# Transformer layer with 64 experts: the last attention taken by query tile, and nine experts' weight loads moved

## The chip, the cores and the metric

One core of a Trainium2 chip runs the whole program. The metric is the device time of one execution in microseconds, as a median over runs. The engines are TensorE (PE), VectorE (DVE), ScalarE (ACT), GpSimd (POOL) and SyncE (SP); SyncE issues the plain transfers, GpSimd the indirect ones.

## The reference

x is 4 x 256 x 256. A modulation from a small matrix gives shift, scale and gate for two sub-layers. Float32 throughout.

```python
h = layernorm(x) * (1 + ca) + sa
x = x + ga * attention(h)            # 16 heads of 16, rotary, causal, 256 x 256 weights
h = layernorm(x) * (1 + cb) + sb
x = x + gb * experts(h)
...
# experts: x has 1024 tokens
probs = softmax(h @ router_weight.T)             # 64 experts
topw, topi = top_k(probs, 8); topw = topw / sum(topw)
pos = rank of each (token, expert) among the expert's tokens, in token order
xe[e, pos] = h (pos < 128 only)                  # capacity 128
y = sum over k of topw * down_e(silu(g) * u),  g, u = split(xe @ gate_up_e)   # 256 -> 2 x 96 -> 256
```

The rank in token order makes the slot number of a token depend on all tokens before it, so the tiles of 128 tokens have their slots made in order.

## The kernel before

A batch is 256 tokens, two tiles of 128 (TPB = 2); there are B = 4 batches, eight tiles. The attention stage is a software pipeline written out by hand for each engine: a round `it` does the second half of batch it - 1 (softmax, values, output projection, second norm, router, top 8, slots) beside the first half of batch `it` (projections, rotary, transposes, and the scores whose maxima the softmax subtracts). Engines meet at semaphores only. Each one's instructions run in the order of the text, so a wait holds all that is written behind it on that engine.

**The last attention** (batch 3) has no batch beside it. On TensorE `attend` (line 943) makes, for each of four groups of four heads, the transposed scores of both query tiles in three chunks (two pairs of heads with 256 queries against key tile 0, and four heads with 128 queries against key tile 1), and one group later the products with the values (L959); ScalarE's `softmax` makes the exponentials (L664) and copies two groups at a time to the SBUF (L671). `att_transposes` (L988) turns the result to tokens by rows, VectorE's `attention_out` divides, `out_transposes` (L996) and `o_proj` (L1005) project, `residual` adds and takes statistics, `rstd` and `finish_rstd` make 1/sqrt, `h2_normalise`, `h2_transposes` (L1013) and `h2_copy` make the modulated norm, `router` (L1029) the logits, `rows_transposes` (L1020) the rows to be scattered, `picks` and `slots` (L1354 to L1388) the top 8 and the slot numbers, with `ranks` (L1038) between them. In this tail the two tiles are handled apart but side by side: on VectorE in the order residual 0, finish 0, residual 1, finish 1, picks 0, slots 0, picks 1, slots 1. `keep_warm` issues products whose result nobody reads (L852): four and two within the tail, 30 after the last slot numbers, and three after the wait for seven tiles' scatters.

**The scatters.** GpSimd writes each tile's rows to the slots of their experts in DRAM with eight indirect transfers (L596), one for each of the eight choices; those of batch 2 run beside the last attention, each behind a wait (`beside_last_attention`) that spaces them out. Transfers of the last tile count on a semaphore of their own (`g_last`), all others on `g_scat`.

**The experts.** For each of 64 experts SyncE loads 128 slot rows (`load_slots`, L448, eight buffers), TensorE transposes them (L1146; for the first five experts, whose slots can hold rows of the last tile, it adds those from the SBUF by a product with a 0/1 matrix, L1143 to L1148), multiplies (L1157), transposes (L1165) and multiplies again (L1171). GpSimd adds the result to one of three sums in DRAM (L616, L619), each add after the one before on the same sum; results wait in a ring of 16. The nine last experts are added by products on TensorE (L1199). At the end the sums are loaded and folded by VectorE.

**The weights.** All experts' weights live in one SBUF tensor, `arena`, whose second half (experts 32 to 63) is scratch of the attention stage until its parts come free. Of experts 32 to 63, seven were loaded at the start of what the last values products free (AFTER_PV = 7: 32 to 38), nine (39 to 47, up to AFTER_QK = 16) after the last slot numbers, and the others before. SyncE's order around this is:

```python
sp.wait_ge(p_pv, 4 * B)
sp.dma_start(code_table, ...)
load_experts(EARLY, AFTER_PV, s_lw[1])
sp.wait_ge(v_slot, B * TPB)
load_experts(EARLY + AFTER_PV, AFTER_QK - AFTER_PV, s_lw[2])
sp.wait_ge(g_scat, 16 * K * (B * TPB - 1))
```

Then come the first five slot loads, the wait for `g_last`, three more, and the rest, each behind the step that frees its buffer.

## Time and profile before

| | us |
|---|---|
| median of 3 runs | 336.37 (331.1 to 338.41) |
| the profiled execution | 329.7 |
| its span, first to last instruction | 327.9 |
| TensorE busy | 288.1 (88%) |
| VectorE busy | 206.2 (63%) |
| ScalarE busy | 158.8 (48%) |
| GpSimd busy | 158.9 (48%) |

The mean granted clock of TensorE is 0.952 of full speed. The span has two stages: the attention, to about 174, and the experts, from 189.73 to the end; between them all computing engines but GpSimd are idle or run products that nobody reads. Busy shares are means over both, so a part of the kernel is judged by the order of time in it. Every time below is in us from the start of the span. An engine's idle time stands in brackets with what ended it; "issue" is time in which it waited for nothing that the profile shows.

### The profile page before, as it was taken

The numbers are of one execution on the slowest core, as the hardware profiler recorded it, in microseconds if no ns is written. First come the engines' busy times: TensorE is split into PE (matmuls) and PEld (weight loads), VectorE is DVE, ScalarE is ACT, GpSimd is POOL, SyncE is SP. The second block draws the span as 40 slices with busy tenths as digits, with TensorE's granted clock in tenths as the row PEclk, the third lists the DMA queues.
The fourth block names the chain that finished last, engine by engine and source line by source line (L and its number), as shares of the span: only waits on it lengthen the run. The fifth ranks groups of instructions, "written<-read, shape, count | busy, mean of one in ns | idle before, by whom it ended". The sixth has DMA issues, their size and how long they took to land.

```text
span 327.9 us, 7233 instructions
## 1 busy us (share of the span) xinstructions
PE 288.1 (88%) x2084; PEld 213.0 (65%) x2084; DVE 206.2 (63%) x640; ACT 158.8 (48%) x461; POOL 158.9 (48%) x156
## 2 busy tenths in 40 slices
PE   7999999899889898969658389999999999999990
PEld 3468477466646674646333089788888887778880
DVE  3296677778677967740552027677767679993186
ACT  3437288428743584436241015566666666592000
POOL 2800000003455455655737732687887788887300
PEclk9998999999999999599967969999999999999997
DMA  7880399999999998812977953699999988866972
GB/s 219 266 274 3 48 335 336 351 381 239 286 308 270 289 241 262 223 69 80 227 212 223 289 155 108 139 152 160 158 156 165 188 148 151 107 72 71 222 239 96
DMA packets 63594, 64.89 MB, mean 198 GB/s; under 512 B 4880, under 2 KB 60375, under 8 KB 63569
## 3 DMA queue, kind: packets, MB, share of 16 engines
q1 hardware_dynamic: 52864, 49.39, 54.3%
q0 software_dynamic: 10704, 15.20, 25.7%
q8 instruction: 12, 0.20, 0.3%
q14 instruction: 14, 0.11, 0.1%
HBM read 36.26 MB, written 28.84 MB: 199 GB/s over the span
## 4 chain that ended last, share of the span: by engine, by line
PE 60%; issue 14%; DVE 9%; DMA 7%; ACT 6%; SPq 2%; POOL 0%; another core or an unknown queue 0%; ACTq 0%; DVEq 0%; POOLq 0%
PE bank L1157 12%; PE bank L1171 7%; PE bank L899 6%; PE bank L1146 3%; PE bank L975 3%; PE bank L911 3%; PE bank L973 3%; PE bank L959 3%; PE bank L930 2%; DMA sum<-kz,stage 2%; PE bank L970 2%; PE bank L927 2%; PE bank L1165 2%; PE bank L1005 2%; DVE arena L1552 2%
## 5 line engine op out<-in xcount | busy, mean ns | idle before, releaser
L596 POOL DMA_INDIRECT slot_rows<-stage x48 | 47.9, 998 | 38.3 <-issue 10.9
L1157 PE MATMUL bank<-arena,stage 128*128 (+1 forms) x256 | 53.5, 331 | 0.6 <-ACT stage L800 0.6
L616 POOL DMA_INDIRECT sum<-kz,stage x26 | 40.1, 1543 | 9.5 <-issue 6.6
L800 ACT ACTIVATE stage<-bank 128x256 f32<-128x256 f32 x64 | 24.6, 384 | 38.1 <-PE bank L1148 22.6
L1157 PEld LDWEIGHTS bank<-arena,stage 128*128 128x128 f32 x256 | 40.3, 191 | 1.7 <-issue 0.8
L1171 PE MATMUL bank<-arena,stage 96*128 (+1 forms) x128 | 40.4, 397 | 0.1
L1299 DVE TENSOR_REDUCE rmax<-bank 128x2 f32<-128x512 f32 (+1 forms) x48 | 30.6, 685 | 5.9 <-PE bank L930 4.6
L616 POOL DMA_INDIRECT sum<-stage x17 | 26.4, 1554 | 6.8 <-issue 5.0
L664 ACT ACTIVATE arena<-bank 128x512 f32<-128x512 f32 x48 | 26.7, 599 | 6.0 <-PE bank L975 5.3
L583 POOL COPY stage<-slot_idx 128x16 uint32<-128x16 uint32 x2 | 0.4, 197 | 59.9 <-DVE slot_idx L1388 59.9
L899 PE MATMUL bank<-arena 128*128 128x512 f32 (+1 forms) x64 | 25.8, 528 | 2.9 <-ACT arena L647 2.9
L852 PE MATMUL bank<-onesb 128*128 128x512 bf16 x67 | 21.3, 474 | 7.7 <-DMA slot_rows<-rows,slot_idx 4.9
L1510 DVE SCALAR_TENSOR_TENSOR stage<-stage,bank 128x96 f32<-128x96 f32 x64 | 16.2, 253 | 16.8 <-ACT stage L810 11.2
L975 PE MATMUL bank<-stage 128*128 128x256 bf16 (+1 forms) x128 | 24.6, 246 | 0.0
L973 PE MATMUL bank<-arena,kz 128*128 128x256 f16 (+1 forms) x128 | 24.6, 246 | 0.0
L807 ACT ACTIVATE stage<-bank 128x96 f32<-128x96 f32 x64 | 16.1, 251 | 17.2 <-PE bank L1157 9.9
L1199 PE MATMUL bank<-arena 128*128 128x256 bf16 x216 | 23.7, 271 | 0.0
L1146 PE MATMUL bank<-cst,stage 128*128 128x128 f32 x118 | 22.9, 275 | 0.1
L1199 PEld LDWEIGHTS bank<-arena 128*128 128x128 bf16 x216 | 20.9, 97 | 2.8
L1171 PEld LDWEIGHTS bank<-arena,stage 96*128 96x128 f32 x128 | 19.1, 189 | 3.9 <-ACT stage L817 0.3
L1146 PEld LDWEIGHTS bank<-cst,stage 128*128 128x128 f32 x118 | 16.2, 141 | 7.5 <-issue 2.1
L596 POOL DMA_INDIRECT slot_rows<-rows,slot_idx x16 | 16.2, 1013 | 9.2 <-DVE slot_idx L1388 4.6
(199 smaller groups left out, 603.2 us busy)
## 6 DMA issues: line engine op xcount, KB each, us to landing
slot_rows<-zero_row SPq DMA_DIRECT2D x8, 1040.0 KB, 12.6
stage<-slot_rows SPq DMA_DIRECT2D x64, 130.0 KB
arena<-in_gate_up SPq DMA_DIRECT2D x8, 768.0 KB
sum<-zero_row SPq DMA_DIRECT2D x3, 1152.0 KB, 12.6
arena<-in_gate_up SPq DMA_DIRECT2D x4, 864.0 KB
arena<-in_down SPq DMA_DIRECT2D x4, 768.0 KB
arena<-sum SPq DMA_DIRECT2D x12, 256.0 KB, 5.3
arena<-in_gate_up SPq DMA_DIRECT2D x4, 672.0 KB
```

Source lines behind the costliest of these rows:

```text
L596: pool.indirect_dma_start(slot_rows, bass.IndirectOffsetOnAxis(ap=idx[:, t, k:k + 1], axis=0), src[:, t, :], None, bounds_check=SLOTS - 1, ...
L616: pool.indirect_dma_start(sums[a], where, ye_ring[e % RING], None, bounds_check=ACCROWS - 1, oob_is_err=True, compute_op=ALU.add).then_inc ...
L664: nc.scalar.activation(dst, bank[4 + n % 3][:, :], ACT.Exp, scale=SCALE).then_inc(a_exp, 1)
L800: nc.scalar.activation(xeT[:, j % 2, :], bank[j % 2][:, 0:HC * CAP], ACT.Copy).then_inc(a_xeT, 1)
L899: mm(dst, h1T[:, k, t * P:(t + 1) * P], wqkv_sb[:, k, c0:c1], start=k == 0, stop=False)
L973: mm(view[:, i, :], kz[:, h, kt * P:(kt + 1) * P], qT[:, h // 2, kt * P:S], start=False, stop=False, skip_group_check=True)
L975: last = mm(view[:, i, :], pickb[:, h, :], negT[:, kt * P:S], start=False, stop=i == len(heads) - 1, skip_group_check=True)
L1146: last = nc.tensor.transpose(dst, xe[:, j, k * P:(k + 1) * P], ident)
L1157: last = mm(bank[2 + q % 2][:, 0:GU + 1], xeT[:, q % 2, k * CAP:(k + 1) * CAP], expert_w[:, s - 1, k * (GU + 1):(k + 1) * (GU + 1)], start ...
L1171: mm(bank[6 + q % 2][:, 0:H], hidT[:, q % 2, :], expert_w[0:I, s - 3, HC * (GU + 1):EW], start=True, stop=True).then_inc(p_ye, 1)
L1199: last = mm(dst, picked[:, n, of:of + P], y[:, n, :], start=n == 0 and y is own_high, stop=n == NPICK - 1 and y is own_low)
L1299: V.tensor_reduce(rmax[:, qt, h0:h0 + 2 * nh - 1:2], src, AX.X, ALU.max).then_inc(v_max, 1)
```

## The change

The last attention goes by query tile. The scores are made in twelve chunks of four heads by 128 queries: four for tile 0 (key tile 0 only), then eight for tile 1. The values, the copy, the transposes, the projection and the residual of tile 0 are issued between tile 1's chunks. Exponentials go to six buffers in place of probT's two groups (`probs_last`). On VectorE tile 0's picks and slots stand ahead of tile 1's residual, on ScalarE its rows and sums ahead of tile 1's estimate. Six warm-up products within the tail are gone; the 30 and the three stay. GpSimd's waits for batch 2's eighth to twelfth scatter name later events. Of the nine experts' weights, four are loaded after tile 1's projection, and five, one by one, behind the first five slot loads of the third round (`load_eight(2, ...)`), which with round 1 is written out of the loop; TensorE waits for these five before step 40, so that round 4 is written out too. `wo_sb` changes places with `rope2` in the scratch, so that what the first 11 late experts overwrite (AFTER_O = 11) is no longer used once the last projection is done.

```diff
...
+        def probs_last(n):
+
+            return probT[:, :, :].rearrange("p a c -> p (a c)")[:, (n % 6) * 512:(n % 6 + 1) * 512]
+
         def tiles(ts):
...
             load_experts(EARLY + AFTER_QK, ANYTIME - AFTER_QK, s_lw[0])
-            sp.wait_ge(p_pv, 4 * B)
+            sp.wait_ge(p_pv, 4 * B + 4)
             sp.dma_start(code_table, code_row.rearrange("o (e c) -> o e c", c=CAP).broadcast_to([P, FIRST, CAP])).then_inc(s_cr, 16)
             load_experts(EARLY, AFTER_PV, s_lw[1])
+            sp.wait_ge(p_o, B + 1)
+            load_experts(EARLY + AFTER_PV, AFTER_O - AFTER_PV, s_lw[2])
             sp.wait_ge(v_slot, B * TPB)
-            load_experts(EARLY + AFTER_PV, AFTER_QK - AFTER_PV, s_lw[2])
...
-            def load_eight(i):
+            def load_eight(i, weights=0):
                 for j in range(GRP):
                     load_slots(i, j, False)
-
-            with sp.Fori(1, 6) as i:
+                    if j < weights:
+                        load_experts(EARLY + AFTER_O + j, 1, s_lw[3])
+
+            load_eight(1)
+            load_eight(2, AFTER_QK - AFTER_O)
+            with sp.Fori(3, 6) as i:
                 load_eight(i)
...
                     pool.wait_ge(p_s2, 12 * c + 2 * n - 3)
-                elif n in (8, 9):
-                    pool.wait_ge(p_pv, 4 * c + n - 5)
+                elif n == 8:
+                    pool.wait_ge(p_o, B)
+                elif n == 9:
+                    pool.wait_ge(p_pv, 4 * c + 7)
                 elif n == 10:
...
                 elif n == 11:
-                    pool.wait_ge(p_attT, B)
+                    pool.wait_ge(p_attT, B + 1)
                 elif n == 12:
-                    pool.wait_ge(p_o, B)
+                    pool.wait_ge(p_o, B + 1)
                 elif n == 13:
...
             one_round(B - 1, False)
-            softmax(B - 1, None)
-            for t in ALL:
-                att_copy((t,), B + t, t)
+
+            def last_exp(n):
+                if n >= 6:
+                    act.wait_ge(p_pv, 4 * (B - 1) + (n - 5 if n < 10 else 5))
+                act.wait_ge(p_s2, 12 * (B - 1) + n + 1)
+                nc.scalar.activation(probs_last(n), bank[4 + n % 3][:, :], ACT.Exp, scale=SCALE).then_inc(a_exp, 1)
+
+            def last_att_copy(t):
+                act.wait_ge(p_pv, 4 * (B - 1) + 4 * (t + 1))
+                nc.scalar.activation(att_sb[:, t, :], bank[(7, 2)[t]][:, :], ACT.Copy).then_inc(a_att, 1)
+
+            for n in range(6):
+                last_exp(n)
+            last_att_copy(0)
+            for n in range(6, 10):
+                last_exp(n)
+            att_copy((0,), B, 1)
+            last_exp(10)
+            last_exp(11)
+            last_att_copy(1)
             rstd((0,), B)
+            att_copy((1,), B + 1, 0)
             h2_normalise(B - 1, (0,), B)
             h2_copy(B - 1, (0,), B, 0)
+            rows_copy(B - 1, (0,), B, 0)
+            exp_sums(B - 1, (0,), B)
             rstd((1,), B + 1)
             h2_normalise(B - 1, (1,), B + 1)
-            rows_copy(B - 1, (0,), B, 0)
-            exp_sums(B - 1, (0,), B)
             h2_copy(B - 1, (1,), B + 1, 1)
...
             one_round(B - 1, False)
-            attend(B - 1)
-            att_transposes(B - 1)
-            for t in ALL:
-                out_transposes(B - 1, (t,), t)
-                o_proj((t,), B + t, t)
-            keep_warm(4, bank[4])
+            def last_scores(n):
+                g, t, kt = (n, 0, 0) if n < 4 else ((n - 4) // 2, 1, n % 2)
+                if n >= 3:
+                    pe.wait_ge(a_exp, 12 * (B - 1) + n - 2)
+                view = bank[4 + n % 3][:, :].rearrange("p (h q) -> p h q", q=P)
+                if t == kt:
+                    mm(view, identb, maskTb[:, None, :].broadcast_to([P, 4, P]),
+                       start=True, stop=False, skip_group_check=True)
+                for i, h in enumerate(groups[g]):
+                    mm(view[:, i, :], kz[:, h, kt * P:(kt + 1) * P], qT[:, h // 2, t * P:(t + 1) * P],
+                       start=t != kt and i == 0, stop=False, skip_group_check=True)
+                    last = mm(view[:, i, :], pickb[:, h, :], negT[:, t * P:(t + 1) * P],
+                              start=False, stop=i == 3, skip_group_check=True)
+                last.then_inc(p_s2, 1)
+
+            def last_values(t, g):
+                pe.wait_ge(a_exp, 12 * (B - 1) + (g + 1 if t == 0 else 2 * g + 6))
+                for kt in range(t + 1):
+                    slot = probs_last(g if t == 0 else 4 + 2 * g + kt)
+                    for i, h in enumerate(groups[g]):
+                        last = mm(bank[(7, 2)[t]][32 * i:32 * i + 32, g * P:(g + 1) * P], v_aug[:, kt, h, :],
+                                  slot[:, i * P:(i + 1) * P], start=kt == 0, stop=kt == t, skip_group_check=True)
+                last.then_inc(p_pv, 1)
+
+            def last_att_transposes(t):
+                pe.wait_ge(a_att, 2 * (B - 1) + t + 1)
+                for g in range(4):
+                    last = nc.tensor.transpose(bank[(0, 5)[t]][:, g * P:(g + 1) * P],
+                                               att_sb[:, t, g * P:(g + 1) * P], ident)
+                last.then_inc(p_attq, 1)
+
+            pe.wait_ge(a_negT, B)
+            for n in range(3):
+                last_scores(n)
+            pe.wait_ge(v_rank, B)
+            last_values(0, 0)
+            last_scores(3)
+            last_values(0, 1)
+            last_scores(4)
+            last_values(0, 2)
+            last_scores(5)
+            last_values(0, 3)
+            last_scores(6)
+            last_scores(7)
+            last_att_transposes(0)
+            last_values(1, 0)
+            last_scores(8)
+            last_scores(9)
+            last_values(1, 1)
+            out_transposes(B - 1, (0,), 1)
+            last_scores(10)
+            last_scores(11)
+            o_proj((0,), B, 0)
+            last_values(1, 2)
+            last_values(1, 3)
+            last_att_transposes(1)
+            out_transposes(B - 1, (1,), 0)
+            o_proj((1,), B + 1, 1)
             h2_transposes(B - 1, (0,), B, 0)
...
             rows_transposes((0,), 0)
-            keep_warm(2, bank[3])
+            ranks((0,), B, 0)
             h2_transposes(B - 1, (1,), B + 1, 1)
-            ranks((0,), B, 0)
             router((1,), B + 1, 1)
...
                 pe.wait_ge(s_lw[n], 16 * 3)
-            with pe.Fori(EARLY // GRP, E // GRP) as i:
+            for j in range(GRP):
+                expert_steps(EARLY // GRP, j, False, False)
+            pe.wait_ge(s_lw[3], 16 * 3 * (AFTER_QK - AFTER_O))
+            with pe.Fori(EARLY // GRP + 1, E // GRP) as i:
                 for j in range(GRP):
...
             one_round(B - 1, False)
             clear()
-            attention_out(B - 1)
-
+            attention_out(B - 1, (0,), (0, 5))
             residual(B - 1, (0,), B, 0)
             finish_rstd((0,), B)
+            attention_out(B - 1, (1,), (0, 5))
+            picks(B - 1, (0,), B, 0)
+            slots(B - 1, (0,), B, 0)
             residual(B - 1, (1,), B + 1, 1)
             finish_rstd((1,), B + 1)
-            picks(B - 1, (0,), B, 0)
-            slots(B - 1, (0,), B, 0)
             picks(B - 1, (1,), B + 1, 1)
...
```

## Rows read from the trace of the kernel before

**Rows 1.** The chain of waits from 140 to 200: start us, us, what.

```profile
158.29 15.24 issue
...
177.48 9.35 issue
186.82 1.88 DMA stage<-slot_rows
```

**Rows 2.** GpSimd's instructions in order of time: start us, us, engine, line.

```profile
165.36 0.97 POOL L596 DMA_INDIRECT slot_rows<-stage  x1 [0.31 <-issue]
170.92 0.97 POOL L596 DMA_INDIRECT slot_rows<-rows,slot_idx  x1 [4.58 <-DVE slot_idx L1388]
...
180.50 0.97 POOL L596 DMA_INDIRECT slot_rows<-rows,slot_idx  x1 [0.30 <-issue]
...
190.72 0.97 POOL L596 DMA_INDIRECT slot_rows<-rows,slot_idx  x1 [0.31 <-issue]
```

**Rows 3.** SyncE's slot loads issued from 192 to 193: duration ns min/median/max.

```profile
L448 SPq DMA_DIRECT2D stage<-slot_rows x1: 328/328/328, 192.8 to 192.8; - x1
```

**Rows 4.** Stretch, us, busy us of PE, PEld, DVE, ACT, POOL, clock, DMA share, GB/s.

```profile
161.00:163.00 2.00, 1.94 (x9) 1.08 (x9) 1.32 (x7) 0.41 (x3) 1.16 (x2) 1.00 1.09 385
...
176.00:177.00 1.00, 1.00 (x4) 0.35 (x3) 0.00 (x0) 0.00 (x0) 0.69 (x2) 0.50 0.80 264
177.00:178.00 1.00, 1.00 (x6) 0.49 (x5) 0.00 (x0) 0.00 (x0) 0.70 (x2) 0.98 1.02 347
...
193.00:194.00 1.00, 1.00 (x8) 1.00 (x6) 0.46 (x3) 0.00 (x0) 0.00 (x0) 0.50 0.15 22
194.00:195.00 1.00, 1.00 (x7) 1.00 (x8) 0.31 (x3) 0.40 (x2) 0.00 (x0) 0.94 0.94 253
...
209.00:212.00 3.00, 2.94 (x18) 2.54 (x18) 2.07 (x9) 1.94 (x8) 2.64 (x2) 1.00 0.73 132
...
221.00:230.00 9.00, 9.00 (x58) 7.99 (x57) 7.20 (x26) 5.83 (x25) 7.18 (x6) 1.00 0.92 156
```

**Rows 5.** GpSimd's first, fifth and last adds, TensorE's late products, columns as rows 2.

```profile
200.88 1.00 POOL L619 DMA_INDIRECT sum<-stage  x1 [8.79 <-DVE stage L1520]
...
209.05 1.57 POOL L616 DMA_INDIRECT sum<-stage  x1 [1.47 <-issue]
...
304.89 1.54 POOL L616 DMA_INDIRECT sum<-kz,stage  x1 [0.30 <-issue]
...
296.03 23.75 PE L1199 MATMUL bank<-arena 128*128 128x256 bf16 x216
```

**Rows 6.** TensorE's instructions in order of time, columns as in rows 2.

```profile
154.92 0.86 PE L959 MATMUL bank<-arena 128*32 128x256 f32 x16 [0.72 <-ACT arena L664]
156.50 1.09 PE L988 MATMUL bank<-cst,arena 128*128 128x128 f32 x8 [0.72 <-ACT arena L671]
...
158.88 1.13 PE L1005 MATMUL bank<-arena 128*128 128x256 f32 x4 [0.47 <-ACT arena L688]
...
163.94 0.44 PE L1013 MATMUL bank<-cst,arena 128*128 128x128 f32 x2 [0.56 <-issue]
...
173.56 8.35 PE L852 MATMUL bank<-onesb 128*128 128x512 bf16 x30 [1.65 <-issue]
...
189.73 0.77 PE L1143 MATMUL bank<-cst,stage 128*128 128x128 f32 x2 [1.80 <-issue]
```

**Rows 7.** Weight loads of line 959, from 143 to 170: count, busy us, mean ns.

```profile
L959 PEld LDWEIGHTS bank<-arena 128*32 128x32 f32 x64 | 1.7, 109 | 2.0 <-ACT arena L664 1.0
```

**Rows 8.** VectorE's instructions in order of time, columns as in rows 2.

```profile
160.26 0.42 DVE L1328 TENSOR_TENSOR arena<-bank,arena 128x256 f32<-128x256 f32 x1 [1.73 <-PE bank L1006]
...
167.48 0.23 DVE L1354 MAX8 top<-bank 128x8 f32<-128x64 f32 x1 [1.16 <-PE bank L1029]
...
169.86 0.17 DVE L1388 TENSOR_SCALAR slot_idx<-code 128x8 uint32<-128x8 f32 x1
...
173.33 0.17 DVE L1388 TENSOR_SCALAR slot_idx<-code 128x8 uint32<-128x8 f32 x1
```

13 lines of the change are left out of this document (7 added, 6 removed).

## The prediction

> **What bounds the kernel now.** I first read the chain of waits around the last attention [rows 1]. From 158.29 it holds no computing engine: SyncE's queue sits still for 15.24 us until the last tile's slot numbers exist, issues the nine late experts' loads, sits still again for 9.35 us until seven of the eight tiles' rows have been scattered, and only then loads the first slots. GpSimd in order of time gives the cause [rows 2]: sixteen scatters of batch 2 run to 166.33, the queue is empty for 4.58 us, and the sixteen of batch 3 start at 170.92, one each 1.28 us, the eighth ending at 181.47 and the last at 191.69. So three things are in series: the tail of the attention, the scatters, and a landing. The landing is read from two places: the eighth scatter ended at 181.47 and SyncE went on at 186.82, 5.35 us later; the last ended at 191.69 and SyncE went on at 192.8, 1.1 us later [rows 1 to 3]. Between the two the traffic differs: the DMA engines were full from 177 on (1.02), and nearly empty at 193 (0.15) [rows 4].
>
> After that the end is set by GpSimd's adds, 55 in all, 1.54 us each with 0.30 between: from 209.05 to 304.89 there are 50 steps of 1.845 us, which is 92.2 of 95.8 us [rows 5]. TensorE ends its late products at 319.78 [rows 5]. Both ends move with the start of the experts.
>
> **Part 1, the attention by query tile.** Scores and values are as much work as before: 12 blocks of 128 columns for each group of four heads, 12 exponentials and two copies of 512 columns on ScalarE. New is the order. Tile 0's transposes, out transposes and projection now stand before tile 1's last values: four and two transposes of 0.11 us (eight take 0.88 and a tail) and 1.17 for the projection with its bias, 1.8 us of TensorE [rows 6]. The last values ended at 155.78; in the new order 157.6. The leg from there until VectorE reads a projection took 155.78 to 160.26, 4.48 us [rows 6, 8]; for tile 1 it has four transposes fewer (0.44) and waits once more: VectorE has finish_rstd of tile 0 ahead of it, whose estimate stands on ScalarE behind the second copy of the attention, which I put at 0.65 us. So tile 1's projection is done at 157.6 + 4.48 - 0.44 + 0.65 = 162.3.
>
> The smaller values products need 96 weight loads in place of 64. The row says 109 ns each [rows 7], and 16 of them lie within the 0.86 us of a group [rows 6], where one after the other they would take 1.74; so they overlap, and I take 0, with 32 x 0.109 = 3.5 us as the other bound. A rule speaks against the change here: the Trainium skill (TensorE: Matmul & The Clock Gate, The mechanism, in the part on packing) has weight loads overlap running products only when the row group differs, and here it is the same; by the rule up to 3.5 us would be paid, and the sum below would be -1.0. The trace does not agree.
>
> **Part 2, tile 0's back half.** Its h2_transposes follow the second projection at once, where they now start at 163.94 behind four warm-up products. From them to the slot numbers it takes until 170.03, 6.1 us, of which 1.16 is a wait before 167.48 that nothing in the trace explains [rows 6, 8]. New: 162.35 + 4.9 to 6.1, so 167.2 to 168.4. GpSimd gets free later: its waits for batch 2 are re-spread, and the twelfth needs tile 1's projection. Add 0.9 (what the first scatter took to start behind slot numbers ready at 170.03) and four scatters, 5.1 us: free at 168.3. So the first scatter of batch 3 starts at 168.3 to 169.3; I take 168.7, 2.2 us earlier. The eighth ends at 168.7 + 7 x 1.277 + 0.97 = 178.6, the last at 188.8.
>
> **Part 3, tile 1's back half** now stands whole behind tile 0's slots on VectorE. From residual to slots it takes 160.26 to 170.03, 9.8 us, for tile 0 now. Without the 1.16 wait and with 0.4 for products at the low clock: 9.0, bounds 8.6 and 10.2 (the wait stays). Last slots: 167.8 + 9.0 = 176.8 (175.8 to 178.6), against 173.50 now [rows 8]. **They become later by 3.3 us**, and what is queued behind them matters: the 30 warm-up products on TensorE, 8.35 us [rows 6], the first of them at the low level of the clock (0.50, 1.2 GHz, until 177; 2.4 GHz after [rows 4]); TensorE will have been as idle before them. GpSimd needs these slots at 168.7 + 10.2 = 178.9 and is not held by them.
>
> **Part 4, the weights.** Four experts (1.2 MB) go out at 162.3 behind the seven that already fill the DMA engines then (1.09 at 161 to 163 [rows 4]); only scatters that nobody waits for share that time. At the eighth scatter's end the engines are quiet, and I take the landing of the quiet case, 1.1 us (bounds 1.1 and 5.35): rows of seven tiles are in at 179.7. TensorE is at its warm-up products until 176.8 + 0.06 + 8.35 = 185.2, and after three more (0.64) starts at 185.9. So the landing leaves the path, but **the warm-up products are late next**. The gain at TensorE's start is 189.73 - 185.9 = 3.8 us (2.1 to 4.8). In exchange no idle lies between them and the experts: at present TensorE runs from 189.73 to 194 at 0.50 [rows 4, 6], 4.3 us that are 2.1 at 1.00. Gain 2.0 (0 to 2.1). Slots 5 and up wait for the last scatter, 188.8 + 1.1, and a load of 1.9 [rows 1]: 191.8, wanted after five steps of 1.5 us or more, 193.4 at the earliest: hidden.
>
> Five experts (1.5 MB) go into the second round of slot loads. Fifteen more issues on SyncE at 0.33 us [rows 3] are 5 us, and the slot loads are eight steps (12 us) ahead, so they hide. The traffic is 1.5 MB at the 347 GB/s of a full stretch [rows 4], 4.2 us of all engines, where they are 0.73 busy and GpSimd waits 1.47 us once already; later they are at 0.92 [rows 4, 5]. An add waits for the one three before it, so a later landing is paid. Bounds 0 and 4.2; I take 1.3, what is left when the idle quarter of 12 us takes its share.
>
> The extra unrolled eight on TensorE and the wait for the fourth weights semaphore cost nothing: the weights are there some 25 steps before. wo_sb changes its place only.
>
> **Sum**, against the profiled execution's own 329.7 us (span 327.9 and 1.8 around it): -3.8 - 2.0 + 1.3 = -4.5, so 325.2. The median of the runs shown is 336.37 (331.1 to 338.41), 6.7 above that execution; the same shift puts the median at 331.8, I say 331.5.
>
> **Rivals.**
> One, all bounds are kind: slots at 175.8 and TensorE at 184.9 (4.8), clock 2.1, no contention, and half a us of the wait before 209.05 goes: 7.4 gained, 329. For it: the 1.16 wait looks like an accident. Against: traffic is not free. Chance 0.22.
> Two, the change moves the first scatter but not the experts: tile 1's tail is long, slots at 178.6 or later, TensorE at 187.6, gain 2.1 + 2.0 - 1.3 = 2.8, 333.6. For it: the clock is low for all of its products. Chance 0.15.
> Three, the weight loads of the values products are not hidden: 3.5 later, gain 1.0, 335.4. Against it stands the row above. Chance 0.05.
> Four, slower: the five loads among the adds. If they make a landing 4.25 us later, as the nine did to the eighth scatter (5.35 against 1.1), a chain of three adds pays it once a round, and the loads span two to three rounds: 8.5 to 12.8 us, less the 5.8 gained before, is 2.7 to 7 slower, 339 to 343. It decides from 1.4 rounds on. Against it: each load is 0.29 MB, not 2.65 at once, with 1.5 us between. Chance 0.08. The Trainium skill (DMA: Bandwidth & Descriptors, Issuing engines are not separate DMA queues) has the transfers of all engines interleave on the same 16, which is what this rival needs.
> The forecast itself: 0.50.
>
> **Numbers.** Runs of this kernel differ by 2% among themselves, and 2% (6.7 us) is about what tells a change from none. Rival one is over it, with some of the forecast's edge: faster 0.27. Rival four is beyond it on the other side: 0.08. The rest, 0.65, is within. Range: the forecast with its bounds is 328.5 to 334; out to rivals one and two and the spread of the runs it is 326 to 337.
>
> **What would show it.** In the changed profile: tile 1's projection at 162 to 163; the first scatter from rows at 168.3 to 169.3, with no gap of 4.6 before it; last slot numbers at 176 to 178; SyncE's first slot load 1.1 us behind the eighth scatter, near 180; TensorE's 30 warm-up products ending after that, and the experts starting at 185 to 187 at a clock of 1.00; 55 adds at 1.85 with no longer waits near the tenth. I am wrong if the warm-up products are not what the experts wait for, if the clock is 0.50 at the experts' start, or if the adds stretch.

## The result, and the profile after

In 20 runs of each, the changed kernel took 336.19 us in the median (331.51 to 338.72) and the kernel before 334.55 (328.66 to 338.41). Some executions of every kernel lie more than 1.5% above its fastest; the ratios here and below leave them out, the medians do not. The ratio is 1.0118, 95% interval 1.0071 to 1.0164: slower by about 4 us (the medians differ by 1.6), where I had forecast 4.5 to 5 us faster. Repeated in three more comparisons the ratio was 1.0175 [1.0111, 1.0239], 1.0144 [1.0063, 1.0224] and 1.0216 [1.0139, 1.0294]. The profiled execution took 337.46 us with a span of 335.6 and a mean granted clock of 0.927 (before 329.7, 327.9, 0.952).

The chain of waits of the changed kernel (start us, us, what) already says where to look:

```profile
156.78 3.95 another core or an unknown queue
...
164.49 2.07 PE bank L1035 x4
...
170.79 5.01 issue
...
181.43 10.21 PE bank L882 x33
192.64 0.27 PE bank L1225
192.91 1.83 issue
194.90 1.24 issue
196.31 0.33 PE bank L1224 x2
```

SyncE is gone from it, as intended [rows 1]. In its place stand the warm-up products (L882), which I had forecast, and four pieces in which an engine waits, the first and the last two of which I had not. GpSimd in order of time (start us, us, engine, line), the last scatter of batch 2, the first, eighth and last of batch 3, then the first and last add:

```profile
171.53 0.98 POOL L608 DMA_INDIRECT slot_rows<-stage  x1 [0.30 <-issue]
173.07 0.97 POOL L608 DMA_INDIRECT slot_rows<-rows,slot_idx  x1 [0.56 <-issue]
...
182.03 0.97 POOL L608 DMA_INDIRECT slot_rows<-rows,slot_idx  x1 [0.30 <-issue]
...
192.27 0.97 POOL L608 DMA_INDIRECT slot_rows<-rows,slot_idx  x1 [0.30 <-issue]
...
205.77 1.00 POOL L631 DMA_INDIRECT sum<-stage  x1 [12.13 <-DVE stage L1604]
...
311.09 1.54 POOL L628 DMA_INDIRECT sum<-kz,stage  x1 [0.30 <-issue]
```

The 4.58 us gap ahead of batch 3 is gone [rows 2], yet its first scatter came at 173.07, not 168.7. And from the last scatter's end to the first add it took 12.5 us (205.77 less 193.24), where it had taken 9.2 [rows 2, 5]. SyncE goes on 1.3 us after the eighth scatter's end, as forecast:

```profile
184.31 20.08 SPq L454 DMA_DIRECT2D stage<-slot_rows  x12
```

TensorE in order of time, from the last values to the first experts (L1224 to L1238):

```profile
156.83 1.08 PE L1157 MATMUL bank<-arena 128*32 128x128 f32 x32
...
161.40 1.12 PE L1164 MATMUL bank<-cst,arena 128*128 128x128 f32 x4 [3.49 <-ACT arena L799]
...
181.43 10.21 PE L882 MATMUL bank<-onesb 128*128 128x512 bf16 x33 [1.65 <-DVE slot_idx L1472]
191.48 0.38 PE L1224 MATMUL bank<-cst,stage 128*128 128x128 f32 x2
...
192.15 0.28 PE L1225 MATMUL bank<-kz,rows 128*128 128x128 f32 x1
192.64 0.27 PE L1225 MATMUL bank<-kz,rows 128*128 128x128 f32 x1 [0.22 <-issue]
194.74 0.17 PE L1229 MATMUL bank<-kz 128*128 128x3 f32 x1 [1.83 <-issue]
196.14 0.17 PE L1229 MATMUL bank<-kz 128*128 128x3 f32 x1 [1.24 <-issue]
196.17 0.47 PE L1224 MATMUL bank<-cst,stage 128*128 128x128 f32 x2
```

There are two holes. **Hole B**: inside the first expert TensorE stands still for 0.22, 1.83 and 1.24 us between products that wait for no data and no buffer (the slots are long there); it runs on from 196.14, 2.9 us after the last scatter's end. **Hole A**: the 32 last values products end at 157.9 by their modelled end, but the two engines that wait for their count both go on at 160.75 (ScalarE's copy, and SyncE's load of the code table):

```profile
160.75 0.35 SPq L441 DMA_DIRECT2D kz<-in_code_row  x1
160.75 0.60 ACT L799 ACTIVATE arena<-bank 128x512 f32<-128x512 f32 x1 [3.97 <-remote]
```

So it looks as if TensorE itself was late with the last of them, whose ends the profile only models. The stretches (us, busy of PE, PEld, DVE, ACT, POOL, clock, DMA share, GB/s) show what the clock did then, and the adds:

```profile
161.00:163.00 2.00, 1.12 (x4) 0.72 (x4) 1.05 (x6) 0.64 (x3) 0.00 (x0) 0.50 0.40 106
163.00:176.00 13.00, 5.73 (x18) 3.32 (x19) 4.68 (x22) 3.46 (x10) 8.18 (x9) 0.50 1.04 291
...
182.00:192.00 10.00, 10.00 (x38) 4.27 (x36) 0.28 (x3) 0.00 (x0) 7.81 (x8) 0.73 0.48 145
...
221.00:230.00 9.00, 9.00 (x56) 7.67 (x55) 6.63 (x25) 5.94 (x25) 6.16 (x4) 1.00 1.04 247
```

After hole A the clock is at 0.50 (1.2 GHz) from 161 on, where before it was 1.00 at 161 to 163 [rows 4]; tile 1's projection takes 2.07 us where 1.13 was its price [rows 6]. At 221 to 230 the engines carry 247 GB/s, 156 before [rows 4], which fits the five moved loads.

### The profile page after: what moved, and what is told of

The parts are those of the page before. It is cut to its first block, busy times and chain, and to the rows that moved or that the text cites. A ratio compares the mean times of both kernels' runs of the same rounds, so it can differ in the third digit from the quotient of the medians.

```text
span 335.6 us, 7275 instructions
## 1 busy us (share of the span) xinstructions
PE 288.7 (86%) x2138; PEld 214.8 (64%) x2138; DVE 205.5 (61%) x640; ACT 158.6 (47%) x461; POOL 158.4 (47%) x156
## 4 chain that ended last, share of the span: by engine, by line
PE 60%; DVE 12%; issue 12%; ACT 8%; DMA 5%; another core or an unknown queue 1%; SPq 1%; POOL 0%; ACTq 0%; DVEq 0%; POOLq 0%
PE bank L1238 11%; PE bank L1252 7%; PE bank L929 6%; PE bank L1227 3%; PE bank L882 3%; PE bank L941 3%; ACT arena L676 2%; DMA arena<-sum 2%; PE bank L960 2%; PE bank L1246 2%; PE bank L1059 2%; PE bank L1035 2%; PE bank L957 2%; DVE arena L1636 2%; DVE rmax L1383 2%
## 5 line engine op out<-in xcount | busy, mean ns | idle before, releaser
L1238 PE MATMUL bank<-arena,stage 128*128 (+1 forms) x256 | 54.0, 333 | 0.7 <-ACT stage L830 0.7
L1238 PEld LDWEIGHTS bank<-arena,stage 128*128 128x128 f32 x256 | 40.8, 193 | 1.6 <-issue 1.1
L1252 PE MATMUL bank<-arena,stage 96*128 (+1 forms) x128 | 40.1, 395 | 0.0
L1227 PE MATMUL bank<-cst,stage 128*128 128x128 f32 x118 | 22.8, 274 | 0.0
L882 PE MATMUL bank<-onesb 128*128 128x512 bf16 x61 | 20.4, 500 | 2.7 <-DVE slot_idx L1472 1.7
L676 ACT ACTIVATE arena<-bank 128x512 f32<-128x512 f32 x36 | 20.0, 599 | 3.2 <-PE bank L1005 2.7
L960 PE MATMUL bank<-kz,arena 128*128 128x128 f16 (+1 forms) x128 | 18.9, 255 | 0.0
L1005 PE MATMUL bank<-stage 128*128 128x256 bf16 (+1 forms) x96 | 18.4, 246 | 0.0
L1003 PE MATMUL bank<-arena,kz 128*128 128x256 f16 (+1 forms) x96 | 18.4, 246 | 0.0
```

The lines of the kernel that those rows point to most:

```text
L676: nc.scalar.activation(dst, bank[4 + n % 3][:, :], ACT.Exp, scale=SCALE).then_inc(a_exp, 1)
L882: mm(idle[:, :], onesb, onesb[:, None, :].broadcast_to([P, 4, P]), start=True, stop=True)
L960: last = mm(view[:, i, :], qT[:, h // 2, qt * P:(qt + 1) * P], kz[:, h, 0:w], start=False, stop=i == len(heads) - 1, skip_group_check=True)
L1227: last = nc.tensor.transpose(dst, xe[:, j, k * P:(k + 1) * P], ident)
L1238: last = mm(bank[2 + q % 2][:, 0:GU + 1], xeT[:, q % 2, k * CAP:(k + 1) * CAP], expert_w[:, s - 1, k * (GU + 1):(k + 1) * (GU + 1)], start ...
L1252: mm(bank[6 + q % 2][:, 0:H], hidT[:, q % 2, :], expert_w[0:I, s - 3, HC * (GU + 1):EW], start=True, stop=True).then_inc(p_ye, 1)
```

## The experiments

Single executions start the last attention at different times (138.4 to 146.2 us over all profiles, in no order), so all profiles are compared from t0, ScalarE's copy that opens the last attention (143.99 before, 144.15 after). "Comparison" is one set of kernels timed together with the kernel before; the holes turned out to depend on it.

| kernel | comparison, median of before | median | ratio [95%] |
|---|---|---|---|
| c0, changed again | I, 328.65 | 333.86 | 1.0175 [1.0111, 1.0239] |
| e1, before + weights only | I | 333.26 | 0.9996 [0.9934, 1.0059] |
| e2, attention only | I | 335.80 | 1.0209 [1.0152, 1.0266] |
| e3, 12 late warm-ups | I | 335.33 | 1.0157 [1.0081, 1.0233] |
| e4, slot loads all last | II, 327.81 | 337.62 | 1.0311 [1.0234, 1.0387] |
| e5, 96 instructions more, earlier | II | 332.74 | 1.0195 [1.0107, 1.0283] |
| e6, 180 more, in late warm-ups | II | 337.92 | 1.0299 [1.0198, 1.0400] |
| e7, residual 1 first | II | 333.38 | 1.0168 [1.0076, 1.0260] |
| f1, before + e6's padding | III, 322.89 | 323.28 | 1.0015 [0.9976, 1.0055] |
| f2, 128 more on ScalarE | III | 325.58 | 1.0087 [1.0039, 1.0136] |
| f3, 128 more on TensorE | III | 322.68 | 0.9952 [0.9902, 1.0002] |
| f4, no late warm-ups | III | 318.61 | 0.9847 [0.9787, 0.9908] |
| g0, changed again | IV, 332.58 | 335.97 | 1.0144 [1.0063, 1.0224] |
| g1, f4 again | IV | 330.90 | 1.0083 [1.0012, 1.0153] |
| g2, before, no late warm-ups | IV | 327.29 | 0.9891 [0.9800, 0.9982] |
| g3, e1, no late warm-ups | IV | 334.40 | too spread for a ratio |
| h1, one last scatter of eight | V, 329.41 | 329.48 | 1.0039 [0.9994, 1.0084] |
| h2, changed again | V | 334.92 | 1.0216 [1.0139, 1.0294] |

The steps, in us from t0, each from one profile; "forecast" is the prediction less 143.99, its last two entries following from its sum:

| | before | forecast | after | h2 | h1 | f2 | f3 | f4 | g1 |
|---|---|---|---|---|---|---|---|---|---|
| tile 1's projection done | 18.4 | 18.3 | 22.7 | 22.8 | 22.7 | 18.7 | 18.7 | 18.7 | 22.7 |
| first scatter of batch 3 | 26.9 | 24.7 | 28.9 | 29.0 | 28.9 | 24.6 | 24.6 | 24.6 | 28.9 |
| last slot numbers | 29.5 | 32.8 | 37.2 | 37.3 | 37.2 | 32.9 | 32.5 | 32.5 | 37.2 |
| last scatter's end | 47.7 | 44.8 | 49.1 | 49.1 | 40.1 | 44.8 | 44.8 | 44.8 | 49.1 |
| TensorE's first expert | 45.7 | 41.9 | 47.3 | 47.2 | 45.9 | 41.6 | 41.6 | 38.1 | 42.6 |
| first add | 56.9 | 51.1 | 61.6 | 61.7 | 54.9 | 50.6 | 50.6 | 49.6 | 58.7 |
| last add, less first | 104.0 | 105.3 | 105.3 | 104.1 | 104.3 | 104.3 | 102.9 | 102.9 | 104.4 |

**Which part costs it (c0, e1, e2).** e1 is the kernel before with the weights' part alone (its first four loads wait for the second projection), e2 the changed kernel with the nine loads back behind the last slots:

```diff
+            sp.wait_ge(p_o, B + 1)
+            load_experts(EARLY + AFTER_PV, AFTER_O - AFTER_PV, s_lw[2])
             sp.wait_ge(v_slot, B * TPB)
-            load_experts(EARLY + AFTER_PV, AFTER_QK - AFTER_PV, s_lw[2])
```

> The changed kernel as it is, a second look beside the parts below. Expected ratio to before 1.005 to 1.017. The first profile of it has two holes on TensorE that the prediction did not have: 157.9 to 160.7 behind the last 32 values products, and 192.2 to 196.1 within the first expert. Theory one (instruction supply: TensorE gets its instructions in blocks of 16 KB, and a block arrives at 158) expects both holes again, at the same instructions, their length varying. Theory two (the values products by tile are themselves slower than their records, since their weight loads are not hidden) expects the first hole with the same length and has no reason for the second.

> Only the weights part of the change on the kernel before: four late experts loaded after the last projection, five among the second round of slot loads; attention as before. By the prediction's terms: the eighth scatter still ends at 181.5, its landing shrinks from 5.35 to about 1.2 us, so SyncE goes on at 182.7 in place of 186.8; TensorE's warm-up products end at 181.9; experts start near 185.3 at the full clock; -4.3 at the start, -2 for the clock, +1.3 for the adds: about -5 us, ratio 0.985. If the five loads among the adds cost more than the landing gives (rival four), the ratio is 1 or above.

> Only the attention part: nine experts' weights loaded after the last slot numbers as before. Theory: the attention part is what loses. Last slot numbers at 181 (173.5 before), warm-up products until 191.5, the landing of the eighth scatter (183.0 + 5.35 = 188.4) hidden behind them; experts start at 191.5 or later, no traffic among the adds: ratio 1.01 to 1.02. The rival (the loads among the adds are the loss) expects 0.99 to 1.0 here.

The weights alone, for which I had expected 0.985, show no change by the ratio, which rests on four of its 13 runs (the medians of all runs differ by 4.6 us), though the landing shrinks (to 1.3 us): ScalarE's first expert copy came 2.6 us after the last scatter's end, 0.6 before. The attention alone costs all of the loss. Its adds took 103.0 us against 104.7 in c0; over all profiles the 16 with the moved loads took 104.3 us from first to last add in the mean (102.9 to 105.3), the four without 103.0 (101.7 to 104.0), which prices the moved loads at 1.4 us.

**Are the warm-up products, or the early start, what counts (e3, e4)?** e3 has 12 late warm-up products for 30; e4 holds the first slot loads until the last scatter too (`if j == FIRST` becomes `if j == 0`).

> The changed kernel with 12 instead of 30 warm-up products after the last slot numbers. In the first profile the scatters of seven tiles were in at 184.3 but TensorE was at its warm-up products until 191.5. Theory: 12 at the low level of the clock take 5.1 us, until 186.6, so the experts start near 187.3, 4.2 us earlier, and pay up to 2.2 for the low clock in the first experts: 2 to 4 us faster than the changed kernel, ratio to before about 1.00. If the warm-up products are not what the experts wait for, no gain.

> The changed kernel, with the first slot loads too behind the last scatter (they are issued 10 us later than now). In four profiles of kernels with early first loads ScalarE's first copy of an expert (start of the useful work) came 2.6 to 3.2 us after the last scatter had ended, however early TensorE was ready. Theory one: the first experts do not get through before the last scatters are done, whatever their loads do; then this kernel loses only what a load takes, 0 to 2 us against the changed kernel, ratio to before 1.018 to 1.024. Theory two: the early start is worth what it looks like; then it loses the 7 us between the 8th scatter's landing and the last's, ratio 1.03 or more.

In e3 both first experts' products were through at 188.6, and then ScalarE's copy of the first stood still until 195.77, 2.9 us after the last scatter's end, with 14.96 us of idle put down to "remote". The warm-up products were no longer in the way and nothing came of it. In e4 the first add was 14.7 us behind the last scatter, 12.5 in c0, so by the steps the early start is worth some 2 us. By time it is more: e4's median is 4.2 and 4.9 us above those of e7 and e5 in the same comparison, and its ratio lies where my second theory had it (1.03 or more). Its price lies between 2 and 5 us, and which of the two theories holds is not decided.

**More instructions, the same work (e5, e6).** Both cut warm-up products of 512 columns into four of 128: same columns, more instructions, as each product is a weight load and a matmul. e5 does it to 16 ahead of the last attention (96 more), e6 to the 30 late ones (180 more), in effect:

```diff
-            keep_warm(30, bank[4])
+            for _ in range(120):
+                mm(bank[4][:, 0:P], onesb, onesb, start=True, stop=True)
```

> The changed kernel with the 16 warm-up products of the round before the last attention cut into four of 128 columns each: same time, 48 more products and weight loads, so 96 more instructions ahead of the last attention. Instruction supply (TensorE's 16 KB blocks arrive at 150 and 158 in the first profile) expects the hole behind the last values products (157.9 to 160.7) to move or go, and the block transfers to come some 3 us earlier in the same work; time -3 to +1 us. If the hole belongs to the values products or to the clock, nothing moves.

> The changed kernel with the 30 late warm-up products cut into 120 of 128 columns: same time, 180 more instructions between the attention and the experts. If the stop within the first expert (192.2 to 196.1 in the first profile) is a lack of instructions at a block's end, it moves to another instruction or goes, up to 4 us gained. If it depends on the last scatters, it stays at the first expert and ends about 2.9 us after the last scatter: no gain, ratio 1.015 to 1.02.

e6, TensorE, among its late warm-up products, which read only constants:

```profile
179.78 3.83 PE L887 MATMUL bank<-onesb 128*128 128x128 bf16 x34
184.68 0.26 PE L887 MATMUL bank<-onesb 128*128 128x128 bf16 x1 [1.07 <-issue]
186.79 0.27 PE L887 MATMUL bank<-onesb 128*128 128x128 bf16 x1 [1.84 <-issue]
189.58 0.26 PE L887 MATMUL bank<-onesb 128*128 128x128 bf16 x1 [2.53 <-issue]
190.98 0.26 PE L887 MATMUL bank<-onesb 128*128 128x128 bf16 x1 [1.14 <-issue]
192.37 0.26 PE L887 MATMUL bank<-onesb 128*128 128x128 bf16 x1 [1.12 <-issue]
193.77 2.50 PE L887 MATMUL bank<-onesb 128*128 128x128 bf16 x22 [1.14 <-issue]
```

And the weight loads between them, one for each product (some records are missing):

```profile
190.27 0.10 PEld L887 LDWEIGHTS bank<-onesb 128*128 128x128 bf16 x1 [1.99 <-issue]
191.67 0.10 PEld L887 LDWEIGHTS bank<-onesb 128*128 128x128 bf16 x1 [1.29 <-issue]
193.07 0.10 PEld L887 LDWEIGHTS bank<-onesb 128*128 128x128 bf16 x1 [1.29 <-issue]
```

These rows settle that the hole is no wait for data: the products have no input that could be late. TensorE got one instruction every 0.70 us (load at 190.27, product at 190.98, load at 191.67, product at 192.37), and the full rate again from 193.77, 2.7 us after the last scatter's end (191.03). The steps of hole B in the changed kernel are the same 0.70 us apart (loads at 194.04 and 195.44, products at 194.74 and 196.14). The hole moved to an earlier place in the program, and its end stayed tied to the scatters; the experts started at 58.8 us from t0, and the version is the slowest but one (1.0299).

e5 speaks against a supply in blocks. By that theory its 96 instructions should have moved hole A or closed it, and the block that came at 158.10, 14.0 us from t0, did come earlier (152.69, 10.4 us from t0). Hole A stayed at the same products (3.87 us of idle before ScalarE's copy, 3.97 in the first profile). Hole B came only a few instructions later, at the first products of the second expert, and again ended 2.7 us after the last scatter. What the holes of the changed kernel's four profiles, e5 and e6 have in common is another count: the first slow step stands 80 to 91 recorded instructions behind the first late warm-up product, be they warm-up products or experts'. That fits a stock of instructions that TensorE holds when its wait for the slot numbers ends, and a slow issue of those behind it; it is an argument, and no run separated it.

The trace has the supply of instructions as a queue of its own. Of the profile of the changed kernel, the queue (packets, MB, share of the DMA engines' span) and the stretch between two of its packets, at 150.07 and 158.10 (columns as above):

```profile
q8 instruction: 13, 0.21, 0.3%
```

```profile
150.00:158.00 8.00, 7.91 (x134) 5.90 (x126) 1.68 (x5) 4.68 (x9) 4.07 (x5) 1.00 0.16 55
```

A packet is 16 KB, and 134 products and 126 weight loads lie between these two, a block of some 260 instructions; between the packets beside them lie 181, 229 and 303. The Trainium skill (Runtime: NRT & Kernel Launch, Instruction fetch mechanics) states the same block, 16 KiB or 256 instructions, fetched by a DMA queue of the engine's own while it executes the block before; by that page the fetch is mostly hidden. The trace agrees on the 16 KB and roughly on the count. It does not show that the holes are a fetch come late: the first profile has no packet of this queue between 158.10 and 208.43, e6 none between 158.82 and 198.62, so TensorE got its full rate back without a block landing; and f2 below, without a hole, has none between 157.94 and 196.81 either.

**Order on VectorE (e7).** Tile 1's residual and estimate ahead of tile 0's picks and slots, as before the change.

> The changed kernel with tile 1's residual back ahead of tile 0's picks on VectorE, its finish ahead of tile 0's slots, and its estimate on ScalarE ahead of tile 0's row copy. The prediction's part 3 says that the slots of tile 1 are late since they stand whole behind tile 0's: here they come about 4 us earlier (177 in place of 181), the warm-up products end 4 us earlier, and the first slot loads no longer wait for them. If the warm-up products hold the experts, 3 to 4 us faster than the changed kernel (ratio 1.005); if the experts hang on the last scatters, only what tile 0's slots lose or gain shows: 0, ratio 1.015 to 1.02.

Last slots came at 33.6 from t0 in place of 37.2, the first experts' products at 42.9 in place of 47.3, and the first add at 61.6, the same. TensorE was through with both first experts' products at 188.7, and ScalarE's first copy stood until 195.40, 2.5 us after the last scatter's end. What moves TensorE's start did not move the end, because what stands still goes on only after the scatters.

**Position, chip, and the kernel before (f1 to f4).** f1: the kernel before with e6's 120 products. f2: ScalarE's first wait written 128 times. f3: the ten warm-up products at the start as 74 of 128 columns. f4: neither the 30 nor the three late products.

```diff
-            keep_warm(30, bank[4])
...
-            keep_warm(3, bank[4])
```

> The kernel before, its 30 warm-up products of 512 columns behind the last slot numbers cut into 120 of 128 columns: same columns, 180 more instructions for TensorE's queue, results unread. Theory S (TensorE runs out of supplied instructions during the last scatters and is supplied again only some 2.8 us after the last one has ended): the stop moves from the experts' products, or from where it does no harm, into the warm-up products, single products stand 1.4 us apart there, the experts start at the last scatter's end + 2.5 to 4 or later, and the first add stands 12 to 19 us behind the last scatter's end instead of 9.2: 3 to 9 us slower, ratio 1.01 to 1.03. Rival R (the stop belongs to what the change did to the experts' first steps, such as slots loaded while the scatters run): no stop among the warm-up products here, first add at 9 to 10, ratio 1.00.

> The changed kernel with 128 more instructions at the start of ScalarE's program (its first wait, already met, written 128 times), which shifts where everything later on ScalarE lies in its instruction stream; the start may cost some us, seen in when the last attention begins. If ScalarE's supply is what holds its first expert copy (in three runs it waited for nothing that the trace shows while TensorE's products were done): the copy comes at the last scatter's end + 0.5 or earlier in place of + 3.2, or another ScalarE instruction before it stands still. If only TensorE's supply matters here: the copy stays at + 2.5 to 3.5 and TensorE stops at the same products of the first experts as before.

> The changed kernel, the ten warm-up products at its start (512 columns) replaced by 74 of 128 columns: 128 more instructions ahead of everything on TensorE, results unread, the start perhaps 2 us later. Theory S: TensorE's stop moves by about 128 instructions (from the first experts into the warm-up products or into the third to fifth expert) or goes away; if it goes away the first add stands 9 to 10 us behind the last scatter's end instead of 12.5, 2 to 3 us faster than the changed kernel, ratio 1.005 to 1.01 to the kernel before. Rival R: stop at the same products, first add at 12.5, ratio 1.015 to 1.02.

> The changed kernel without the 30 and the three warm-up products behind the last slot numbers. Theory S: 66 instructions fewer ahead of the experts, so both first experts' products are through long before the last scatter, the clock at 0.50 for them; what stands still then is ScalarE's first copy or TensorE's third expert until the last scatter's end + 2.5 to 3; first add again 11.5 to 13 behind the last scatter, ratio 1.01 to 1.02. Rival W (warm-up products late in the way of the experts, as the prediction had it): TensorE's experts start 8 us earlier and the first add with them by 3 to 5 us, ratio 1.00 or less.

None of the four had either hole, with all scatters in place, so the scatters alone do not make one. f2 in the same views (TensorE, ScalarE's first copy, the last scatter, the first add):

```profile
176.51 8.78 PE L883 MATMUL bank<-onesb 128*128 128x512 bf16 x33 [1.65 <-DVE slot_idx L1473]
185.12 0.38 PE L1225 MATMUL bank<-cst,stage 128*128 128x128 f32 x2
...
186.33 0.38 ACT L831 ACTIVATE stage<-bank 128x256 f32<-128x256 f32 x1 [10.03 <-PE bank L1230]
...
187.32 0.97 POOL L608 DMA_INDIRECT slot_rows<-rows,slot_idx  x1 [0.30 <-issue]
194.11 1.00 POOL L631 DMA_INDIRECT sum<-stage  x1 [5.43 <-DVE stage L1605]
```

ScalarE's copy runs 2.0 us before the last scatter's end, not 3.2 behind it. But all four also shared a comparison in which the kernel before was faster than in any other (322.89), and the unchanged changed kernel was not in it; my expectation of f1 (a hole in the kernel before) and of f3 (a hole moved) failed or could not be read.

**The same kernel in two comparisons (g0, g1), and what the late products cost (g2, g3).** g2 and g3 leave the late products out of the kernel before and of e1.

> The changed kernel again, beside the variant without late warm-up products. Theory S (the position of instructions in the stream decides): both stops are there, first add 12 to 12.5 us behind the last scatter's end, ratio 1.012 to 1.018. Rival C (chip or placement decides): no stop in this or in the variant if this chip is like that of the last comparison, first add 5.8 behind the last scatter's end, ratio 0.99 to 1.00.

> The changed kernel without the 30 and three late warm-up products, again. Theory S: as in the last comparison, no stop, first add 4.8 us behind the last scatter's end, ratio 0.98 to 0.99. Rival C: like the changed kernel beside it in where it stops; without stops 0.98 to 0.99, with stops 1.01 to 1.02 as the variant with 12 warm-up products had.

> The kernel before without its 30 and three late warm-up products. Before, these end at 181.9 and the experts wait for the slot loads until 189.7, so only the clock can change: three products fewer behind the wait, up to 0.6 us earlier, the clock low until about 1 us later. Both theories of the warm-up products (in the way or not) give 0.995 to 1.005 here.

> The kernel before with only the weights' loads moved, without the late warm-up products. The landing of 5.35 us is gone, and with the products out of the way the experts' first product comes some 3.3 us after the eighth scatter's end: if nothing stands still, first add 5 to 6 us behind the last scatter's end in place of 9.2 (before) and 11.65 (weights alone), less 1.3 for the adds: ratio 0.985 to 0.995. If ScalarE or TensorE stands still until the last scatter's end + 2.7: ratio 0.995 to 1.005.

g1 is f4's program. In f4 ScalarE's first copy waited for TensorE alone and ran at 184.25, 4.4 us before the last scatter's end:

```profile
184.25 0.39 ACT L830 ACTIVATE stage<-bank 128x256 f32<-128x256 f32 x1 [8.10 <-PE bank L1227]
```

In g1 TensorE's products for it had ended at 187.3, and it ran at 192.29, 0.8 us after the last scatter's end; TensorE's L1236 waited behind it:

```profile
192.29 0.38 ACT L830 ACTIVATE stage<-bank 128x256 f32<-128x256 f32 x1 [12.75 <-remote]
192.73 1.66 PE L1236 MATMUL bank<-arena,stage 128*128 128x193 f32 x4 [3.31 <-issue]
```

So the holes come and go with the comparison, not with the program: the rival, not my theory that the place of an instruction decides. The place decides only where a hole bites. Without the late products the changed kernel gained 5.1 us by the medians of comparison IV (335.97 to 330.90), 2.0 by the ratios, whose intervals overlap. g2 gained too, 1.1% [0.2, 2.0], which I had put at nothing; its profile shows no reason (first add 9.0 behind the last scatter, 9.2 before), so why stays open. g3's first copy was on time (184.08), its second waited 6.17 us for nothing that the trace shows, until 2.2 us after the last scatter's end (188.40): the second case of my expectation.

**Is it the scatters (h1, h2)?** h1 leaves out seven of the last tile's eight scatters (their rows are missing for all but the first five experts), and SyncE's wait for the last tile asks for the one that is left; h2 is the changed kernel beside it.

```diff
-                    for k in range(K):
+                    for k in range(1 if (b, t) == (B - 1, TPB - 1) else K):
```

> The changed kernel with one of the last tile's eight scatters; the other seven are left out, so their rows are missing for slots beyond the first five experts. Theory S (scatters hold the supply of instructions until about 2.8 us after the last one): the last scatter ends some 9 us earlier, before TensorE's warm-up products end, so no stop stands among the first experts: no gap over 1 us between TensorE's products from its start of the experts on, ScalarE's first copy 1 to 2.6 us after the first product, first add 8 to 9 us after TensorE's start, in place of 14.3 (changed kernel); 5 to 6 us faster than it. Rival L (the nine weights' loads or the slot loads hold the supply): the stop stays among the first experts, first add 12 us or more after TensorE's start.

> The changed kernel again. Theory S: if the kernel before is near 330 here, the stops are there (first add 12 to 13.5 us behind the last scatter's end) and the ratio is 1.012 to 1.018; if it is near 323, no stops, first add 5.8 behind the last scatter's end, ratio 0.99 to 1.005. Rival P (the variants' other placement of instructions cured it): stops and 1.012 to 1.018 in either.

h2's TensorE stands still at the same products as the first profile's, until 2.9 us after the last scatter's end (191.37):

```profile
190.77 0.27 PE L1225 MATMUL bank<-kz,rows 128*128 128x128 f32 x1 [0.39 <-issue]
192.86 0.17 PE L1229 MATMUL bank<-kz 128*128 128x3 f32 x1 [1.83 <-issue]
194.27 0.17 PE L1229 MATMUL bank<-kz 128*128 128x3 f32 x1 [1.24 <-issue]
```

h1 has none of it, with the last scatter's end at 183.72:

```profile
189.50 0.38 PE L1224 MATMUL bank<-cst,stage 128*128 128x128 f32 x2
189.72 0.39 PE L1225 MATMUL bank<-kz,rows 128*128 128x128 f32 x2
...
190.71 0.38 ACT L830 ACTIVATE stage<-bank 128x256 f32<-128x256 f32 x1 [10.03 <-PE bank L1229]
...
198.49 1.00 POOL L631 DMA_INDIRECT sum<-stage  x1 [14.37 <-DVE stage L1604]
```

From TensorE's first expert to the first add it took 9.0 us, 14.5 in h2, and the median is 5.4 us lower. Hole B needs the scatters: shown, by one profile of each and medians of the same comparison. Its price in the changed kernel is about 5 us, with whatever the scatters' own traffic cost in it.

## Why the prediction was wrong, by its steps

- **Part 4, start of the experts: the step that failed.** I wrote that TensorE "starts at 185.9" and that the start moves the end by 3.8 us, plus 2.0 for the clock. I took for granted that an engine whose data are there runs. In all four profiles of the changed kernel it did not: TensorE stood still or got single instructions inside the first expert until 2.8 to 2.9 us after the last scatter, so from the first expert to the first add it took 14.3 us, where 11.15 before and 9.2 in the forecast. That is 5.1 of the 10.5 us by which the first add missed the forecast (61.6 against 51.1 from t0); without the seven scatters (h1) it took 9.0.
- **Part 1, the leg from the last values to tile 1's projection.** Forecast 18.3 from t0; 22.7 in the profile. The last values were where I put them (13.8 by their modelled end, forecast 13.6), so the 4.4 us are hole A (3 us) and the low clock behind it. It passes whole into the first scatter (28.9 against 24.7), the last (49.1 against 44.8) and the last slots (37.2 against 32.8), and with the 10.2 us of warm-up products, forecast at 9.0, makes TensorE's start 5.4 late: the other half of the miss. The cause of hole A stays open: f2 to f4 have neither hole, but a block of instructions arrives at the same products there (157.94 in f2), and in e5, where it arrives 3.5 us earlier in the attention, hole A is unchanged. In c0, g0, h1 and h2 the place of hole A is taken by a low clock at the start of the last attention (0.66 to 0.83 in the 10 us from 140, 1.00 in the profile of after) and the sum is nearly the same in h1 and h2 (first scatter at 28.9 and 29.0 from t0) and a third of it in c0 and g0 (26.2 against the forecast's 24.7).
- **Where no hole was, the forecast of the steps holds.** f2 is the changed kernel but for 128 met waits at its start: projection 18.7 (18.3), first scatter 24.6 (24.7), last scatter 44.8 (44.8), last slots 32.9 (32.8), TensorE's experts 41.6 (41.9), first add 50.6 (51.1). So parts 1 to 3 and "the warm-up products are late next" were sized right for a kernel without holes. The time shows the gain only in part: f2 was 0.9% slower than the kernel before (1.0039 to 1.0136), f3 0.5% faster, within its interval's reach of none, and f4, without the late products, 1.5% faster. In the profiles of that comparison the last attention opened at 143.5 to 143.9 in f2 to f4 and at 138.4 in f1, the kernel before with padding; f2's and f3's padding at the start may be part of that, but f4 has none, and it is not explained. The unchanged changed kernel was never seen in that state.
- **Part 3.** Tile 1's back half took 9.3 us (172.09 to 181.37), forecast 9.0. Right.
- **The landing.** 5.35 us became 1.3, forecast 1.1; with the weights back (e2) it was 5.9. Right, and of little use.
- **Contention.** 105.3 us from first to last add against 104.0, and 1.4 more in the mean of all profiles, forecast +1.3. Right, and the rival of 2.7 to 7 us did not come.
- **Weight loads of the values products.** The 96 loads of the last attention (count, busy us, mean ns):

```profile
L1157 PEld LDWEIGHTS bank<-arena 128*32 128x32 f32 x96 | 2.2, 109 | 0.8 <-issue 0.2
```

  They were busy for 2.2 us in all, 96 times 109 ns being 10.5, and the last values ended as forecast. No 3.5 us were paid.

The end moved from 183.9 to 191.5 from t0, 7.6 us in these two profiles: last scatter 1.4 later, first add another 3.3, adds 1.3, and 1.6 behind the last add. The medians differ by less (1.6 us, and by the ratio 4): these two executions lie apart by more than their kernels. That the median of 336.19 lies inside my range of 326 to 337 says little for the forecast: the range was wide, it started from a median of three runs that was 1.8 us above that of twenty, and the sign was wrong.

What stays open: by what path the scatters hold up TensorE's and ScalarE's instructions, whether it is their transfers or GpSimd's work for them that does it, and why the holes are there in one comparison and not in another on chips of the same number (III and IV).

Of what ran, two versions beat the kernel before: f4 (the changed kernel without late warm-up products), 0.985 in III but 1.008 in IV, and g2 (the kernel before without them), 0.989 [0.980, 0.998], run once. Neither is proven across comparisons; in both, late products that read nothing useful were better left out.

## What to carry to other kernels

That data and buffers are ready does not say that an engine runs. When a plan pulls straight-line work of one engine into a stretch where another engine's indirect transfers follow each other without a gap, look for rows with "issue" between products that read only constants, and check whether they end with the transfers: if so, an earlier start there buys little. Filler products took part in that stretch too (e6, and f4 and g1 without them): time the kernel without them before adding more. And time a change of 1% in more than one comparison before believing either sign.

## What the hardware showed that I had not expected

- Single instructions 0.70 us apart on TensorE, and ScalarE copies 5.0 to 7.2 us behind the products they wait for (g1, e7, e3), both until 0.8 to 2.9 us after the last of a chain of indirect transfers.
- The same program at a median of 318.6 and 330.9 us, and the kernel before at 322.9 and 332.6, in two comparisons on chips of the same number.
